# A mixture-of-experts kernel: block tokens in a ring of their own, and two accumulators from block 33 on

## What is computed

```python
h = _rms(x, ff_ln_w)
logits = h @ wg
topv, topi = jax.lax.top_k(logits, TOP_K)
gate = jax.nn.softmax(topv, -1)
weights = jnp.zeros_like(logits).at[bidx, sidx, topi].set(gate)
a = jax.nn.silu(jnp.einsum('bsd,edh->bseh', h, w1)) * jnp.einsum('bsd,edh->bseh', h, w3)
y = jnp.einsum('bseh,ehd->bsed', a, w2)
moe = jnp.einsum('bsed,bse->bsd', y, weights)
return x + moe
```

## Time and profile before

| | us |
|---|---|
| median of 3 runs | 519.99 |
| lowest, highest | 519.49, 520.69 |
| profiled execution: its time | 519.2 |
| profiled execution: its span in the trace | 517.4 |
| TensorE busy (matmuls) | 486.7 |
| VectorE busy | 356.2 |
| GpSimd busy | 270.7 |
| ScalarE busy | 215.9 |

### The profile page before, as it was taken

The page is one execution under the profiler, slowest core; times in us unless marked ns, Lnnn a source line. Parts: engine busy times, 40 slices in busy tenths (PEclk is TensorE's granted clock), DMA queues, the critical chain, the costliest instruction groups (busy, mean ns, idle before and its releaser), DMA issues.

```text
span 517.4 us, 9264 instructions
## 1 busy us (share of the span) xinstructions
PE 486.7 (94%) x2965; PEld 411.8 (80%) x2965; DVE 356.2 (69%) x694; ACT 215.9 (42%) x476; POOL 270.7 (52%) x279
## 2 busy tenths in 40 slices
PE   7899999998989999999999999888799998999877
PEld 3788888887776898989798989776378887878765
DVE  3534241235888989999989898986488666666575
ACT  1322223224333333343343433434177566777660
POOL 2686611104686626252565556655235576777660
PEclk9999999999999999999999999999999999999998
DMA  8988789999642020101030312977786556666578
GB/s 281 306 271 275 249 255 340 339 340 341 190 142 64 1 52 2 42 0 42 3 86 0 92 37 64 341 260 262 254 259 101 99 98 102 97 103 99 94 145 254
DMA packets 67137, 82.53 MB, mean 159 GB/s; under 512 B 20993, under 2 KB 57090, under 8 KB 67074
## 3 DMA queue, kind: packets, MB, share of 16 engines
q1 hardware_dynamic: 56338, 61.16, 39.4%
q0 software_dynamic: 10752, 20.78, 17.9%
HBM read 45.54 MB, written 33.24 MB: 152 GB/s over the span
## 4 chain that ended last, share of the span: by engine, by line
PE 54%; DVE 15%; DMA 14%; issue 7%; POOL 4%; ACT 3%; SPq 1%; POOLq 0%; ACTq 0%; DVEq 0%
PE ringA L1464 19%; PE wide L1464 14%; PE ringT L1464 11%; DMA moe_acc<-y,xs 6%; DMA xs<-moe_rows 4%; DVE z L1137 4%; PE ringT L1572 3%; PE wide L1882 3%; DVE oT_lo L1117 2%; POOL moe_acc L728 2%; DMA staging<-in_cond_w 1%; DVE qs L1055 1%; DVE qc L1055 1%; DMA head_hi<-in_cond_head 1%; PE wide L1849 1%
## 5 line engine op out<-in xcount | busy, mean ns | idle before, releaser
L728 POOL DMA_INDIRECT moe_acc<-y,xs x45 | 82.5, 1832 | 55.4 <-ACT y L739 42.1
L592 POOL TENSOR_TENSOR qr<-qc,qs 128x256 f32<-128x256 f32 x80 | 56.9, 736 | 34.7 <-DVE qs L1055 33.5
L1464 PE MATMUL ringT<-ew,xsT_hi 128*128 (+1 forms) x188 | 60.3, 402 | 0.5 <-DVE xsT_lo L1336 0.5
L1464 PE MATMUL ringA<-qkvw_hi,hT_hi 128*128 128x512 f32 x96 | 40.7, 424 | 4.2 <-DVE qs L1055 3.5
L635 POOL DMA_INDIRECT moe_rows<-hx,slot x32 | 32.8, 1026 | 15.1 <-issue 8.1
L1464 PE MATMUL ringA<-qkvw_hi,hT_lo 128*128 128x512 f32 x96 | 37.7, 392 | 0.0
L1464 PE MATMUL ringA<-qkvw_lo,hT_hi 128*128 128x512 f32 x96 | 37.6, 391 | 0.0
L1464 PE MATMUL ringT<-ew,xsT_lo 128*128 (+1 forms) x94 | 37.0, 394 | 0.0
L1464 PEld LDWEIGHTS ringT<-ew,xsT_hi 128*128 128x128 f32 x188 | 32.0, 189 | 4.9 <-DVE xsT_lo L1336 0.8
L1351 DVE TENSOR_TENSOR w_lo<-ew,w_hi 128x512 fp32r<-128x512 f32 x31 | 21.5, 692 | 20.0 <-ACT w_hi L738 20.0
L1464 PE MATMUL ringA<-wo_hi,oT_hi 128*128 128x256 f32 x112 | 34.8, 310 | 0.0
(11 more groups left out here) (303 smaller groups left out, 1515.5 us busy)
## 6 DMA issues: line engine op xcount, KB each, us to landing
moe_rows<-fill SPq DMA_DIRECT2D x8, 2208.0 KB, 19.7
ew_raw<-in_expert_w SPq DMA_DIRECT2D x16, 512.0 KB, 5.9
xs<-moe_rows SPq DMA_DIRECT2D x47, 138.0 KB, 2.6
staging<-in_cond_w SPq DMA_DIRECT2D x8, 576.0 KB, 4.1
cw_hi<-in_cond_w POOLq DMA_DIRECT2D x8, 576.0 KB, 5.5
v_blk<-v SPq DMA_DIRECT2D x32, 128.0 KB, 3.4
ew<-in_expert_w SPq DMA_DIRECT2D x16, 256.0 KB, 6.4
qkvw_hi<-in_qkv_w POOLq DMA_DIRECT2D x6, 512.0 KB, 5.6
```

What stands on the lines that cost most here:

```text
L592: last = pool.tensor_tensor(rot[:, :, f, :], cos[:, :, f, :], sin[:, :, 1 - f, :], ALU.add)
L728: pool.indirect_dma_start(out=acc_dram[ACC[b]], out_offset=bass.IndirectOffsetOnAxis(xs[:, b % XSR, TOKEN:TOKEN + 1].bitcast(I32), 0), in_ ...
L1464: mm = pe.matmul(out, a, b, start=first and i == 0, stop=last and i == 2, skip_group_check=True)
```

## The change

- After VectorE has made `xsT_lo` of a block, it copies the block's token numbers (a column of 128x1) into a column of a new ring `tok` with 16 columns. This is done for blocks 0 to 44.
- GpSimd's accumulate takes its targets from `tok`.
- SP, ahead of the load into a slot of `xs`, waits for `y_done` of the block that had it, where it waited for that block's accumulate to land.
- `LATE` becomes 47 - 8 - 6 = 33 (it was 39): two arrays in turn from block 33 on, and the third holds no block after 32. The four loads of the third array wait for the landings of blocks 32, 34, 36 and 38 (before: 38, 39, 40 and 41).

```diff
-LATE = NBLK - XSR
+LATE = NBLK - XSR - 2 * NACC
+TOKR = 16
...
+        tok = sb("tok", [P, TOKR], I32)
...
                 if b >= XSR:
-                    old = b - XSR
-                    sp.wait_ge(y_out[ACC[old]], 16 * NTH[old])
+                    sp.wait_ge(y_done, b - XSR + 1)
...
             for h in range(NT // 2):
-                b = LATE + h - 1
+                b = LATE - 1 + 2 * h
                 sp.wait_ge(y_out[ACC[b]], 16 * NTH[b])
...
                 pool.indirect_dma_start(out=acc_dram[ACC[b]],
-                                        out_offset=bass.IndirectOffsetOnAxis(xs[:, b % XSR, TOKEN:TOKEN + 1].bitcast(I32), 0),
+                                        out_offset=bass.IndirectOffsetOnAxis(tok[:, b % TOKR:b % TOKR + 1], 0),
...
             def rows_lo(b):
                 dve.wait_ge(xsT_hi_done, b + 1)
                 dve.tensor_tensor(**lo_part(xsT_lo[:, b % 2, :], xs_bank[b % 2], xsT_hi[:, b % 2, :])).then_inc(xsT_lo_done, 1)
+                if b < SENT:
+                    dve.tensor_copy(tok[:, b % TOKR:b % TOKR + 1], xs[:, b % XSR, TOKEN:TOKEN + 1].bitcast(I32))
```

## The result

Of the changed kernel 20 runs were timed, and of the kernel before 20 in all, the three shown ahead among them. Medians: 518.86 us against 523.52; the ratio is 0.9916, with a 95% interval from 0.9893 to 0.9939. The change makes the kernel 0.84% faster, 4.4 us, where 5.8 were forecast. The time itself, 518.86, lies above the range of 512.2 to 517.2, and 4.7 us above the 514.2 forecast: 3.5 of these 4.7 us are the base, as the three runs of before with their 519.99 were among the fastest of the twenty.

The account below looks back on a forecast made before the run. TensorE, busy 94% of the span, was taken as nearly the bound. Stalls of -7.15 us, lags of 1.4 and 1.3, relief of 1 and copies of +0.1 gave -5.8: from 519.99, 514.2 us, range 512.2 to 517.2.

Parts of the forecast that it names:

- Part 1, the wait: SP waits for y_done, not the landing, so row loads leave earlier and stalls between blocks 21 and 46 vanish: -7.15 us.
- the spare time of 3.1 us: Row loads: wanted 8.65 us after y, there after at most 5.55, so 3.1 us left even with the slowest load.
- Part 2, the copies: VectorE's 45 copies of 128x1 mostly hide in its idle time: +0.1 us, bounds 0 and 0.3.
- The rival in which GpSimd holds the copy: VectorE's copy is held while GpSimd writes descriptors; at 1.6 us a copy the kernel takes 537 us; chance 0.02.
- Part 3: GpSimd reads its 128 targets from `tok` instead of `xs`: cost 0, bounds -0.2 and +0.2 us.
- Part 4, the lag of the pair: Two accumulators from block 33 on make GpSimd wait for block b - 2's landing: 1.4 us of lag, bounds 0 and 9.1.
- the wake of 0.95 us: GpSimd's delay between a landing and its next start, taken between 0.76 and 1.1 us, making each link 5.25 us.
- The estimate of 2.3 us: Skill page's time for one 128 KB accumulate DMA; by it links would never be late and the sum would be -7.0.
- Part 5, the burst: Three third-accumulator loads leave together near 481 us and delay an accumulate: 1.3 us, bounds 0 and 2.6.
- Part 6, the end: Block 44's accumulate starts 4.9 us earlier and the last loads crowd less, so the DMA side ends 5.9 us earlier.
- The relief of 1 us for the last loads: At the end the two accumulators' landings lie apart, so their last loads crowd less: 1 us, from 0 to 1.

Follow-up runs that it names:

- e8_loads_last: Changed kernel with the third accumulator's four loads issued only after block 43's accumulate has landed; ratio to the kernel before 1.0047.
- a2_after: The changed kernel run again without any edit, in the third batch; ratio to the kernel before 0.9905.
- a0_after: The changed kernel run again without any edit, in the first batch; ratio to the kernel before 0.9912.
- e3_five_copies: Changed kernel with each block's column of tokens copied five times, to columns of their own; ratio to the kernel before 0.9934.

## Why the prediction was right or wrong, point by point

- **Part 1, the wait.** Right in its mechanism and in where it ends: no transposes wait for rows, pairs are 2.54 us apart, and the spare time of 3.1 us is confirmed from both sides by seven and six slots. Its size was read from one execution with many stalls. -7.15 us is what that one had; the three profiles of the kernel before have 7.15, 6.21 and 4.79, a mean of 6.05. This is the step that failed: the term was taken from one execution as if every one had it, and was 1.1 us too large, more than any other term.
- **Part 2, the copies.** Right: +0.05 to +0.18 us from block 0 to block 21 for the +0.1 forecast, 143 ns a copy for 146. The rival in which GpSimd holds the copy is out. The rule of the Trainium skill, page "SBUF — State Buffer", section "Who interferes with whom", on copies in a two-port mode, is not seen at work on a column of 128x1; whether this copy runs in such a mode no run here shows.
- **Part 3.** Right as far as seen: lines 728 and 729 have the same durations, 2.01 us at the median.
- **Part 4, the lag of the pair.** Wrong: 1.4 us were put down, 0 to 0.3 is what e8_loads_last shows. Blocks 34 to 39 of the changed kernel start within 0.5 us of their time. What failed here is the wake of 0.95 us after a landing, which was added to every link. At 2.54 us a block GpSimd is still busy with the block between, until 2.54 + 2.01 = 4.55 us after its start for b - 2, when that one lands at 4.3 and so releases nobody; a wake shows only where GpSimd had stood idle, as in a2_after, where block 38 lands at 487.1 and block 40 starts at 488.00. The estimate of 2.3 us by the Trainium skill's page "DMA: Bandwidth & Descriptors", section "Anatomy of one DMA — SWDGE (gpsimd) path", would have given the right answer for a wrong reason: the landings that can be read take 3.5 us and more, with a median of 4.2 in the kernel before.
- **Part 5, the burst.** Right in place and cause, too low in size: block 40 is 1.92 to 2.54 us late in all five profiles of the changed kernel, where 1.3 was forecast. Block 38's accumulate took 6.2 us from start to landing in a0_after and 6.4 in a2_after, against a median of 4.3; in the other three its landing can't be read.
- **Part 6, the end.** The lag at block 44 was 1.3, 1.45, 1.72, 1.72 and 2.68 us, so 4 and 5 together gave nearly the 2.7 foreseen on one chip and 1.3 to 1.7 on the others (mean 1.77). The relief of 1 us for the last loads isn't to be seen: from block 44's accumulate to the end it is 14.1 to 14.8 us in the three profiles before and 13.8 to 14.9 in the five after, 0.2 us less in the mean.
- **The sum.** On two chips both kernels have a profile with block 0 at the same time. There the ends are 517.24 - 512.11 = 5.13 and 515.65 - 511.50 = 4.15 us apart: 6.20 and 4.78 less in the stage, 0.70 and 0.46 more behind it, and the rest, 0.37 and 0.17, ahead of it, about half of that from the copies. By the means of all profiles the stage gives 6.05; the copies take 0.1, the lag 0.97 (1.77 for the 0.80 that the kernel before has), and the last loads give 0.2: 5.2 us. The 4.4 us of the ratio, with its interval of 3.2 to 5.6, agree with both. Against the forecast of 5.8 the stage and the relief of the last loads were too hopeful by 1.1 and 0.8 us, and the lag too dark by 0.9, so part of these errors cancel, which is luck.
- **The time.** The range stood on 519.99, a median of three runs. The twenty have 523.52. The change was forecast as 514.2 / 519.99 = 0.989, and 0.9916 was measured; but a range of 5 us in absolute time had no room for a base whose median was 516.98 us on one chip and 523.4 on another. The 3.5 us of the base weigh more than the error of any term.

## What to carry to other kernels

A wait on a DMA's landing can be replaced by the wait on its source's last reader if the little that the DMA still needs from the buffer is copied away; work out the spare time from reader to next use, and whole periods of it say how many buffers may go. A chain through two buffers that just keeps pace has next to no reserve: most of what a burst of loads costs it stayed to the end here, and moving the burst moved the cost or made it larger. Count stalls in more than one execution before they go into a sum, and give the forecast of a small gain as a ratio rather than a time.

## What the runs showed that was not expected

One and the same program reaches block 0 5 to 6 us later on two of the chips than on the others. Where it is late, most profiles have a stretch of 6.8 to 10.2 us with TensorE at 1.2 GHz at 300 or 350 us (from the granted clocks of windows of 5 or 10 us), and all have one wait of VectorE of 2.2 to 2.4 us that nothing on this core ends; e3_five_copies has the wait without the stretch and is still 4 us late. So the cause stays open. GpSimd's accumulate has mostly one of two lengths in the rows, 1.55 and 2.01 us, and the short ones land earlier too: in the kernel before 3.8 us after their start at the median for 4.3, and 0.3 to 0.6 us apart in seven other profiles whose landings can be read. What decides between them stays open. And 225 copies of a column, five a block, cost TensorE next to nothing: 0.3 us ahead of block 21, and none behind it.
